# Attention kernel: the halves of keys and v move behind the last score product of four steps, and the planner's durations are rewritten

## The reference, cut to what matters

```
scores = einsum('bhqd,bhkd->bhqk', q, k) * scale      # k and v repeated for the 4 heads of a kv head
attn   = softmax(where(causal, scores, -1e9))
out    = einsum('bhqk,bhkd->bhqd', attn, v)           # then out @ Wo.T
return x + attention(xn) + ffn(xn)
```

## Time and profile before

| what | value |
|---|---|
| median of 3 runs | 2233.33 us (2232.9 to 2233.84) |
| the profiled execution's own time | 2236.64 us |
| its span, first to last instruction | 2234.8 us |
| PE busy | 2201.1 us, 98% |
| DVE busy | 1609.4 us, 72% |
| ACT busy | 1129.3 us, 51% |
| POOL busy | 945.3 us, 42% |
| mean granted TensorE clock | 0.998 |

### The profile page before, as it was taken

How to read it: one execution, slowest core, us unless ns; L and a number is a source line. 1 busy time by engine, 2 the same in 40 slices (tenths; PEclk the granted TensorE clock), 3 DMA queues, 4 the chain that set the end, 5 groups by cost and what they waited for, 6 DMA issues and landing times.

```text
span 2234.8 us, 33748 instructions
## 1 busy us (share of the span) xinstructions
PE 2201.1 (98%) x11776; PEld 1304.0 (58%) x11776; DVE 1609.4 (72%) x3732; ACT 1129.3 (51%) x2232; POOL 945.3 (42%) x807
## 2 busy tenths in 40 slices
PE   8999999999999999999999999999999999999998
PEld 6667575765555555555555555555555555555554
DVE  5665554546778787878777777878787878777765
ACT  3323425344555555555455555555555555555644
POOL 4001010102545455555455545555454555455542
PEclk9999999999999999999999999999999999999999
DMA  5756568487111102010202131211101010202000
GB/s 198 287 158 231 201 167 278 160 300 262 29 45 37 55 22 58 24 57 20 62 18 62 44 100 53 72 52 29 57 20 57 24 57 20 62 22 60 15 29 20
DMA packets 82088, 196.89 MB, mean 88 GB/s; under 512 B 9216, under 2 KB 25984, under 8 KB 75264
## 3 DMA queue, kind: packets, MB, share of 16 engines
q1 hardware_dynamic: 79808, 190.55, 27.2%
q10 hardware_dynamic: 2112, 4.19, 0.5%
HBM read 148.57 MB, written 46.14 MB: 87 GB/s over the span
## 4 chain that ended last, share of the span: by engine, by line
PE 90%; DVE 4%; issue 2%; ACT 2%; DMA 1%; POOL 1%; DVEq 0%; SPq 0%; ACTq 0%
PE ob L1418 17%; PE scores L1390 15%; PE qb L1368 13%; PE ob L1429 13%; PE ptb L1402 11%; PE ring L1124 8%; PE ring L1144 8%; PE down L1155 4%; PE ring L1181 2%; DVE acc L1339 1%; ACT short_prob L1262 1%; DVE q_sin L1317 1%; DMA ff_raw<-in_ffw 1%; ACT oT L1279 1%; DVE q_cos L1319 1%
## 5 line engine op out<-in xcount | busy, mean ns | idle before, releaser
L1276 ACT ACTIVATE pT<-ptb 128x512 f16<-128x512 f32 x576 | 332.5, 589 | 343.9 <-PE ptb L1402 342.2
L1418 PE MATMUL ob<-pT,v 128*128 128x512 f16 x1728 | 437.9, 379 | 1.2
L1323 DVE SCALAR_TENSOR_TENSOR pT<-ptb,pT 128x512 f16<-128x512 f32 x576 | 390.3, 687 | 54.8 <-ACT pT L1276 46.9
L1241 POOL TENSOR_TENSOR long_prob<-long_prob,rinv 128x384 f32<-128x384 f32 (+3 forms) x256 | 303.3, 1200 | 132.7 <-DVE rinv L1346 132.6
L1429 PE MATMUL ob<-wo,oT 128*128 128x512 f16 x1536 | 352.9, 379 | 3.6 <-DVE oT L1327 3.6
L1247 POOL TENSOR_TENSOR q_cos<-q_cos,q_sin 128x512 f32<-128x512 f32 x124 | 157.5, 1270 | 461.3 <-DVE q_cos L1319 461.3
L1368 PE MATMUL qb<-xT,wq 128*128 128x512 f16 x1488 | 349.1, 379 | 0.0
L1241 POOL TENSOR_TENSOR short_prob<-short_prob,rinv 128x512 f32<-128x512 f32 (+3 forms) x256 | 276.1, 1094 | 156.8 <-DVE rinv L1346 156.8
L1390 PE MATMUL scores<-kT,late_qT 128*128 128x384 f16 (+3 forms) x1536 | 313.0, 340 | 5.3 <-DVE nmax L1302 4.7
L1262 ACT ACTIVATE long_prob<-long_prob,nmax 128x384 f32<-128x384 f32 (+3 forms) x256 | 204.8, 800 | 183.1 <-DVE nmax L1302 180.3
L1262 ACT ACTIVATE short_prob<-short_prob,nmax 128x512 f32<-128x512 f32 (+3 forms) x256 | 190.8, 745 | 154.7 <-DVE nmax L1302 154.7
(11 more groups left out here) (119 smaller groups left out, 2751.3 us busy)
## 6 DMA issues: line engine op xcount, KB each, us to landing
wq<-w_halves SPq DMA_DIRECT2D x126, 256.0 KB, 3.2
ff_raw<-in_ffw SPq DMA_DIRECT2D x56, 384.0 KB, 5.9
w_fetch<-in_wqo SPq DMA_DIRECT2D x16, 1024.0 KB, 7.1
w_fetch<-in_wqo SPq DMA_DIRECT2D x32, 512.0 KB, 4.8
w_halves<-w_parts SPq DMA_DIRECT2D x32, 512.0 KB, 3.1
wo<-w_halves SPq DMA_DIRECT2D x16, 1024.0 KB, 5.0
k_rows<-stage SPq DMA_DIRECT2D x128, 64.0 KB, 1.7
v_rows<-stage SPq DMA_DIRECT2D x32, 256.0 KB, 2.3
```

The source lines that it names most:

```text
L1241: nc.gpsimd.tensor_tensor(prob[n % 2][:, h, 0:W], prob[n % 2][:, h, 0:W], rinv[:, hd % 8:hd % 8 + 1].broadcast_to([P, W]), ALU.mult)\
L1276: nc.scalar.activation(pT[:, t % 4, HI], ptb[t % 2][:], ACT.Copy, scale=P_SCALE).then_inc(pT_hi, 1)
L1323: nc.vector.scalar_tensor_tensor(pT[:, t % 4, LO], ptb[t % 2][:], P_SCALE, pT[:, t % 4, HI], ALU.mult, ALU.subtract).then_inc(pT_split, 1)
L1418: mm = nc.tensor.matmul(ob[:], v16[e % 2][:, x, j], pT[:, t % 4, y], start=(j == 0 and (x, y) == (HI, HI)), stop=(is_last(kind, n, j) and ...
```

## The change

Nothing is computed differently. The change does two things to the plan: `pieces_split` hangs the four halves on S j = 3 of places 5, 6, 7 and of place 0 of the next group, in place of S j = 0 of places 4 to 7; and the written-in durations of `followers` and `product_cost` get new values. The semaphores are the same.

```diff
--- before.py
+++ after.py
@@ -74,7 +74,7 @@
 W_TOP = 16384.0
 Q_SHIFT = 1.0 / 16384.0
 SCORE_SCALE = -1.0 / (X_SCALE * Q_SHIFT)
-K_UNITS, V_UNITS = (4, 5), (6, 7)
+PIECES = {(5, 3): ("K", 0), (6, 3): ("K", 1), (7, 3): ("V", 0), (0, 3): ("V", 1)}
 FF_SLOTS = 4
 TINY = 1e-25
 FLOORS = (1e-9, TINY, 1e-9)
@@ -196,26 +196,24 @@
 
     cols = key_blocks(n) * P / 1000
     if kind == "S":
-        return [("dve", "S", n, j, 1.04 * cols + 0.08, 0.1), ("act", "EXP", n, j, 0.98 * cols + 0.15, 0.2),
-                ("dve", "INV", n, j, 0.12, 0.06), ("pool", "NORM", n, j, 1.83 * cols + 0.03, 0.05)]
+        return [("dve", "S", n, j, 1.04 * cols + 0.14, 0.14), ("act", "EXP", n, j, 0.98 * cols + 0.28, 0.08),
+                ("dve", "INV", n, j, 0.09, 0.1), ("pool", "NORM", n, j, 1.83 * cols + 0.06, 0.1)]
     if kind == "Q":
-        return [("dve", "Q", n, j, 1.97, 0.05), ("pool", "Q", n, j, 1.1, 0.1),
-                ("act", "QL", n, j, 0.55, 0.1), ("pool", "QL", n, j, 1.1, 0.1)]
+        return [("dve", "Q", n, j, 2.02, 0.08), ("pool", "Q", n, j, 1.24, 0.1),
+                ("act", "QL", n, j, 0.56, 0.1), ("pool", "QL", n, j, 1.13, 0.1)]
     if kind == "W":
-        return [("dve", "W", n, j, 0.61, 0.1)]
+        return [("dve", "W", n, j, 0.66, 0.1)]
     if kind == "T" or is_last(kind, n, j):
-        return [("act", kind, n, j, 0.53, 0.08), ("dve", kind, n, j, 0.61, 0.1)]
+        return [("act", kind, n, j, 0.54, 0.1), ("dve", kind, n, j, 0.62, 0.1)]
     return []
 
 
 def pieces_split(kind, n, j):
 
-    ge, pos = n // TB + 1, n % TB
-    if kind == "S" and j == 0 and ge < B * KVH:
-        for units, hi, lo in ((K_UNITS, "KH", "KL"), (V_UNITS, "VH", "VL")):
-            if pos in units:
-                half = units.index(pos)
-                return [("act", hi, ge, half, 0.6, 0.1), ("dve", lo, ge, half, 0.95, 0.1)]
+    ge = n // TB + (n % TB > 0)
+    if kind == "S" and (n % TB, j) in PIECES and 0 < ge < B * KVH:
+        what, half = PIECES[n % TB, j]
+        return [("act", what + "H", ge, half, 0.6, 0.1), ("dve", what + "L", ge, half, 0.95, 0.1)]
     return []
 
 
@@ -242,11 +240,11 @@
 
 def product_cost(kind, n, j):
     if kind == "S":
-        return max(3 * key_blocks(n) * P * 0.00045, 0.33)
+        return 3 * key_blocks(n) * P / 2400 + 0.01
     if kind in ("QF", "Q"):
         part = q_part(kind, n)
-        return (part[1] - part[0]) * 0.68
-    return {"T": 0.44, "PV": 0.72, "W": 2.72}[kind]
+        return (part[1] - part[0]) * 0.648
+    return {"T": 0.436, "PV": 0.648, "W": 2.592}[kind]
 
 
 def orders():
```

## The result

The changed kernel took 2250.33 us in the median of 4 runs (2249.73 to 2251.08), the kernel before 2233.59 in the same comparison: a ratio of 1.0075, interval 1.0063 to 1.0087. **It is slower by 0.75%, and the forecast was slower by 0.30%, 2239.9 us, with 2244.5 as the upper end of the range.** The direction and the mechanism that was named came true. A second wait, which the prediction had ruled out in a sentence, costs more (0.72 us a group) than the first one adds (0.44).

A forecast was written before the change was run, and what follows sets the result against it. TensorE was taken to bound the kernel; 15 groups x 0.44 us = +6.6 us, opening and tail at zero, took the profiled 2236.64 us to 2243.2 and the median 2233.33 to 2239.9 us (+0.30%), range 2228.0 to 2244.5.

The forecast's parts named there:

- the mechanism that was named: POOL, place 4: normalising of head 0 goes ahead of the query split, so head 3's score product waits; 0.44 us a group.
- What bounds the kernel: TensorE, busy 2201.1 of 2234.8 us; its one recurring wait, behind `nmax` at place 4, loses 0.49 us a group.
- Part 1: Halves moved to idle DVE stretches cost nothing; place 4's score product starts earlier, gaining about 0.3 us a group, 4.5 us.
- Part 2: Planner's order at place 4: both parts of the change together put POOL's normalising of head 0 ahead by 0.31.
- What that costs: Place 4, head 3's score product: PE loses 0.9 us inside it instead of 0.49 before it; 0.43 to 0.44 us a group more.
- Another wait shows up once a group: Sign that the forecast is wrong: a further recurring PE wait besides some 15 for POOL's `late_qT`.
- the first picks of DVE behind the query stay: Other places, steps 0 to 3 and 5 to 7: DVE's first picks keep their order by the hand schedule.
- (a): Rival, POOL at place 4: query split stays ahead of normalising head 0; 2228.8 us, 2226.4 at best; chance 0.21.
- (b): Rival: the swap comes, but gains in opening, tail or other places pay for it; 2234 us, within 0.2%; chance 0.16.
- (d): Rival: new waits let TensorE's clock fall, 1.7 us each on top, giving 2265 us; chance 0.05.
- the prediction's own upper bound of 0.94: Price per group in us of the POOL swap at place 4 if head 0's reciprocal stays at its old time.

The follow-up runs named there:

- pieces_only: The kernel before with the halves of keys and v at their new places and the old written-in durations: 2230.46 us, ratio 0.9976.
- act_swap: The changed kernel with place 4's head 2 exponential (ACT) and reciprocal (DVE) put back ahead of the output copy: 2239.05 us, ratio 1.0018.
- both_swaps: The changed kernel with the edits of act_swap and pool_swap together: 2229.59 us, ratio 0.9977.
- plan_sees: The changed kernel, with the planner told that score products of places 0 and 4 wait for POOL's query split: 2253.99 us, ratio 1.0084.
- pool_swap: The changed kernel with POOL's query split put back ahead of its normalising of head 0 at place 4: 2237.41 us, ratio 1.0011.

## Why the prediction was right and wrong

**What bounds the kernel**: right. The only wait that recurred was the one behind `nmax`, the key half on DVE made it, and both vanish with the half (pieces_only).

**Part 1, the halves move**: right. At their new places they cost nothing. PE doesn't wait for them in pieces_only. In the changed kernel the key halves take 0.74 us on average in place of up to 1.17:

```profile
L520 DVE SCALAR_TENSOR_TENSOR kT<-k,w_scale,kT 128x512 f16<-128x512 f32 x32 | 23.7, 741 | 0.0
```

The gain of this part alone was put at 0.3 us a group and is 0.23, since the rest at T4.0 is 0.22 and not about 0.16 (0.46 less 0.3). One premise was luck: POOL is not quiet at the first of the new places, as the last section shows. The half starts 0.17 us ahead of POOL's normalising there, and it is POOL that is held up.

**Part 2, the order on POOL**: right. NORM4.0 stands ahead of QL7, it takes both parts of the change, and with the gain of part 1 taken off it costs 0.44 us a group (act_swap), as forecast. POOL's split starts 4.90 us behind W2.0's start, where the prediction's 1327.20 - 1322.29 gives 4.91.

**The step that failed** is one sentence of "What that costs": "Behind it: NORM4.3 needs S4.3's pass (DVE about 1328.9, ACT, INV4.3 about 1331.0), ends about 1332.4, and T4.0 would come at 1333.0, so no second wait." It takes the order of ACT and DVE behind S4.3 as it was. I had followed the new plan only up to the pick on POOL, and then let the chip's old order run on. The same plan also turns PV3.0 and head 2 round, on both queues. PE doesn't wait at S4.3 in the plan, so PV3.0's product comes early: counted from the start of S4.0, its copy is ready for ACT at 7.15 us and EXP4.2 at 7.21, ACT is idle, and takes the first. With the old numbers they are ready at 7.54 and 7.31. On the chip PV3.0's product comes 0.9 us later than the plan would have it (it ends at 1333.45, 7.86 us behind S4.0's start, and at 6.95 in the plan), and head 2 stands behind it. In act_swap, where this pair is back in the old order, the sentence is true: NORM4.3 ends 0.6 us ahead of T4.0. The turned pair is worth 0.72 us a group (after against act_swap), 10.8 us in all, against a forecast miss of 2250.3 - 2239.9 = 10.4 us. "Another wait shows up once a group" was the prediction's own sign of being wrong.

A check would have caught it: the claim "the first picks of DVE behind the query stay" was about the first picks of each step, and the pair that turned is the ninth and tenth of place 4 on DVE. On ACT, PV3.0 and head 2 are ready within 0.2 us of each other in the old plan, which is where a plan with new numbers turns first.

**The rivals.** (a), QL7 stays ahead, did not come, and where it was made to (both_swaps, pieces_only) the time was 2229.6 and 2230.5 (ratios 0.9977 and 0.9976) against the 2228.8 given (2228.8/2233.33 = 0.998). (b) came in small: the new order shortens the opening by 1.3 us, within the 3 us that the prediction allowed and took at zero, and no gain at another place of a group shows. That doesn't pay for the swap. (d), the clock falls at each wait, did not come: two waits a group of 0.91 and 0.67 us, and the granted clock stays 1.00 from 600 to 2160 us.

```profile
600.00:2160.00 1560.00, 1541.41 (x8679) 873.72 (x8678) 1204.77 (x3061) 850.67 (x1770) 823.08 (x704) 1.00 0.15 44
```

**The range** had 2244.5 as its upper end. That is 0.75 us a group over 2233.3, less than the prediction's own upper bound of 0.94, which gives 2247.4; and 2250.3 lies beyond both. It had no term for a second pair that turns. A group's length goes from 104.28 to 105.89 us over the orders tried here, so each pair is worth 0.2 to 1.0 us a group, or 3 to 15 us: one more such term was the honest width.

## What to carry to other kernels

When a change feeds new numbers to a planner, compare every pair in the new order with the old, not only those at the place the change is for. Most that turn cost nothing (here three pairs of some twenty did, at two places), but one can cost whatever it waits for, since these queues take their work in the order of `ORDERS` and stop at its head. A plan that leaves out a wait of the real kernel (here POOL's query half) is wrong twice: at the wait, and in all that it orders behind it as if the wait weren't there; adding the wait mends the clock of the plan but not its greed (plan_sees). Put two parts of a change to the chip one at a time: here one gains 0.24%, one nothing, and both together lose 0.75%.

## What the runs showed that I had not expected

ACT and DVE, idle 49% and 28% of the time, delay TensorE at 98% by the order of two instructions in their queues: 0.72 us of each 105. And a wait is not passed on in proportion: pool_swap took 0.91 us of waiting away at S4.3 and all 0.67 us at T4.0 remained.

The prediction took the key half's 1.17 us for contention with POOL and looked for places where POOL is quiet. In the changed kernel a half runs beside POOL's normalising and takes 0.73 us; but the normalising takes 2.11 us, where the one before it, of the same size, takes 1.68. DVE, then POOL:

```profile
1348.73 0.73 DVE L520 SCALAR_TENSOR_TENSOR kT<-k,w_scale,kT 128x512 f16<-128x512 f32 x1
```

```profile
1345.81 1.68 POOL L1239 TENSOR_TENSOR long_prob<-long_prob,rinv 128x896 f32<-128x896 f32 x1 [2.15 <-DVE rinv L1344]
1348.90 2.11 POOL L1239 TENSOR_TENSOR long_prob<-long_prob,rinv 128x896 f32<-128x896 f32 x1 [1.41 <-DVE rinv L1344]
```

In plan_sees the same half comes while such a normalising already runs (the row is two of them, 1.68 us each, the second until 1351.65), and it is the half that takes longer, 1.00 us. DVE, then POOL:

```profile
1351.20 1.00 DVE L521 SCALAR_TENSOR_TENSOR kT<-k,w_scale,kT 128x512 f16<-128x512 f32 x1
```

```profile
1348.33 3.32 POOL L1240 TENSOR_TENSOR long_prob<-long_prob,rinv 128x896 f32<-128x896 f32 x2 [2.08 <-DVE rinv L1345]
```

In before it is the half too: POOL's sum had begun ahead of it, and keeps its length.

```profile
1323.91 1.27 POOL L1247 TENSOR_TENSOR q_cos<-q_cos,q_sin 128x512 f32<-128x512 f32 x1 [3.34 <-DVE q_cos L1319]
```

In all 15 groups of these three kernels it is this way: the one of the two that starts second takes longer, by the overlap less 0.14 to 0.20 us (0.43 us for 0.62 in before, 0.43 for 0.57 in after, 0.25 for 0.45 in plan_sees). An overlap of 0.16 us (the half of v at the end of a normalising, in after) costs nothing. So a busy POOL does not settle what a half costs. What counts is which of the two starts first, and whether PE waits for the one that is held up.
